# Preparation and edge pass of a four-layer graph network in one program, with five more slots for gathered rows

## The reference

```python
h = maximum(layernorm(x), 0)
msg_input = concatenate([h[src], h[dst], edge_attr], axis=-1)
m = relu(msg_input @ W1.T + b1) @ W2.T + b2
agg = segment_sum(m, dst)
y = h + relu(agg @ Wu.T + bu)
x = x + layernorm(y) * gamma + beta
```

## Time and profile before

| | us |
|---|---|
| median of 3 runs | 1938.01 (1937.61 to 1939.03) |
| the profiled execution, its span | 2170.3 |
| difference to the median | 232.3 |
| start of the gathers of PHL (POOL, L399) | 75.8 |
| end of VectorE's work in the preparation | 117.2 |
| first product of the edge pass (PE, L1309) | 128.5 |
| first and last gather of the edge pass (POOL, L989) | 130.6 and 1345.0 |

### The profile page before, as it was taken

One profiled execution on the slowest core, in us unless ns is written; L12 is line 12 of the kernel. 1 busy time (PEld: TensorE's weight loads), 2 busy tenths in 40 slices (PEclk: granted clock), 3 DMA queues, 4 the chain that ended last, 5 costly groups with the idle time before them and its releaser, 6 DMA issues. The chain is left out here.

```text
span 2170.3 us, 30067 instructions
## 1 busy us (share of the span) xinstructions
PE 1378.5 (64%) x9130; PEld 904.1 (42%) x9130; DVE 1129.6 (52%) x3500; ACT 812.2 (37%) x3272; POOL 841.7 (39%) x877
## 2 busy tenths in 40 slices
PE   3235444445445454545545445799899999899997
PEld 2123233333333333333333333356656666455444
DVE  7756666667667666666666666431442224311101
ACT  2235455555545555454545544111343432100000
POOL 5636666666666666666666665000000000000001
PEclk8566766666666666666665666899999999899999
DMA  6444434434443433434434443103100001871770
GB/s 198 143 96 116 115 113 116 122 115 121 121 116 112 122 120 114 118 113 122 119 112 117 120 119 103 30 12 139 34 29 1 10 7 39 305 266 65 264 293 29
DMA packets 200853, 245.67 MB, mean 113 GB/s; under 512 B 36794, under 2 KB 174053, under 8 KB 200674
## 3 DMA queue, kind: packets, MB, share of 16 engines
q1 hardware_dynamic: 142978, 137.56, 20.1%
q0 software_dynamic: 29472, 65.73, 11.7%
q10 hardware_dynamic: 28224, 40.15, 5.2%
HBM read 174.00 MB, written 55.93 MB: 106 GB/s over the span
## 5 line engine op out<-in xcount | busy, mean ns | idle before, releaser
L989 POOL DMA_INDIRECT arena<-dram_PHL,src_of x786 | 765.2, 974 | 472.1 <-remote 205.4
L1327 PE MATMUL psum<-arena 128*128 128x150 f16 x1568 | 238.9, 294 | 604.3 <-DVE aw_out L1034 330.4
L1327 PEld LDWEIGHTS psum<-arena 128*128 128x128 f16 x1568 | 153.4, 125 | 762.2 <-issue 380.6
L1228 ACT ACTIVATE arena<-psum 128x512 f16<-128x512 f32 x202 | 121.9, 603 | 429.3 <-remote 294.5
L1236 ACT ACTIVATE arena<-psum 128x150 fp8e4<-128x150 f32 (+1 forms) x588 | 173.6, 295 | 181.4 <-remote 93.8
L1241 ACT ACTIVATE arena<-psum,arena 128x150 f16<-128x150 f32 (+1 forms) x588 | 228.6, 389 | 1.6 <-remote 1.6
L1309 PE MATMUL psum<-arena 128*128 128x128 f16 x1612 | 182.2, 281 | 39.0 <-DMA arena<-dram_QHL 36.3
L1054 DVE SCALAR_TENSOR_TENSOR agg_all<-psum,agg_all 128x64 f32<-128x64 f32 x202 | 43.8, 217 | 283.4 <-remote 281.4
L1314 PE MATMUL psum<-arena 128*128 128x512 f16 x404 | 184.5, 552 | 3.6 <-issue 3.6
L1244 ACT ACTIVATE aw_out<-psum 128x150 f32<-128x150 f32 (+1 forms) x588 | 179.6, 305 | 0.0
L1043 DVE SCALAR_TENSOR_TENSOR arena<-psum,arena 128x512 f16<-128x512 f32 x202 | 137.9, 683 | 76.2 <-issue 41.3
(11 more groups left out here) (344 smaller groups left out, 2080.3 us busy)
## 6 DMA issues: line engine op xcount, KB each, us to landing
dram_aw<-aw_out ACTq DMA_DIRECT2D x196, 200.0 KB
arena<-dram_aw SPq DMA_DIRECT2D x6, 6400.0 KB
arena<-dram_aw SPq DMA_DIRECT2D x3, 4800.0 KB
arena<-in_ea_quads SPq DMA_DIRECT2D x51, 256.0 KB
arena<-dram_rel SPq DMA_DIRECT2D x51, 256.0 KB
arena<-arena SPq DMA_DIRECT2D x408, 32.0 KB
arena<-dram_PHL,src_of POOLq DMA_INDIRECT x806
arena<-dram_aw SPq DMA_DIRECT2D x2, 4000.0 KB
```

Of the source, the lines that this page charges most:

```text
L989: nc.gpsimd.indirect_dma_start(gathered_p[:, slot, k, :], None, d["PHL"], bass.IndirectOffsetOnAxis(ap=src_of[:, b:b + 1], axis=0)).then_i ...
L1327: done = nc.tensor.matmul(thirds[:, :, i * PKEY:(i + 1) * PKEY], hot_lo[:, u, p, :], hot_key[:, u, p], start=True, stop=True)
```

## The change

One block holds both parts: `prepare` returns five functions that `edge_pass` calls at the head of each engine's program, and the barriers between them are gone. The semaphores of the preparation live on. The preparation's buffers are laid out anew, in strips that the matrix of counts reaches only in later steps. Products and parts have three buffers, and `add_bias`, `copy_p` wait for the stores of group c - 3.

POOL's gathers have ten slots at the start: groups 0 to 4 and then 10, 11, ... use the five of before, groups 5 to 9 five more, once, over the memory of x after h0's stores have landed.

On VectorE `degrees` (in steps 0 to 5), `out_of_bands` (10, 11), `reach` (12, 13) and `badness` (14 to 21) are moved into the loop, each instruction waiting for the end of the one before (`linked`). The degrees are turned round by PE at step 5, stored and loaded back by SyncE at its step 4; folding is at step 8 in place of 2. `row_fields` works with one operation on `past` (f16) and one on the keys where there were two on the keys; `ea_low` comes earlier, `rel_of` is copied by ScalarE, and the squares of the weights come ahead of `ea_high`.

```diff
+AHEAD_P = 5
...
+    d["ahead_p"] = halves[:, H_FIRST:H_FIRST + AHEAD_P * slot].rearrange("p (a b f) -> p a b f", b=MB, f=2 * D)
...
+def slot_of(d, g):
+    if SLOTS_P <= g < SLOTS_P + AHEAD_P:
+        return d["ahead_p"][:, g - SLOTS_P]
+    return d["s_gathered_p"][:, g % SLOTS_P]
...
-        pq = sb("pq", [P, 2, GT, 2, D], F32)
-        hl = sb("pq_parts", [P, 2, GT, 2, 2, D], F16)
+    pq = sb("pq", [P, 3, GT, 2, D], F32)
+    hl = sb("pq_parts", [P, 3, GT, 2, 2, D], F16)
...
 # gpsimd, end of the preparation
-                for g in range(SLOTS_P):
-                    for k in range(blocks_of(g)):
-                        ...
-                pool.wait_ge(rows_in, 16 * PCOLS)
...
 # vector, row_fields
-                    step(nc.vector.tensor_scalar(rows[:, :, :, A_KEY], rows[:, :, :, A_KEY], base[:, 0:1], None,
-                                                 ALU.subtract))
-                    step(nc.vector.scalar_tensor_tensor(out=rows[:, :, :, A_KEY], in0=past[:, :, :], scalar=OUTSIDE,
-                                                        in1=rows[:, :, :, A_KEY], op0=ALU.mult, op1=ALU.add))
+            step(nc.vector.tensor_scalar(past, past, OUTSIDE, base[:, 0:1], ALU.mult, ALU.subtract))
+            dve.wait_ge(pair_rows, 16 * PCOLS)
+            step(nc.vector.tensor_tensor(rows[:, :, :, A_KEY], rows[:, :, :, A_KEY], past, ALU.add))
...
 # vector, end of the preparation's order
-                low_weights()
-                out_of_bands()
-                add_bias(6)
-                low_parts(6)
+        low_weights()
+        add_bias(6)
+        row_lengths()
+        low_parts(6)
...
+        row_fields()
+        ea_low(0)
+        for n, col in enumerate(range(1, PCOLS, 2)):
+            ...
+        ea_low(1)
...
-                degrees()
-                ea_low(0)
-                ea_low(1)
-                reach()
-                badness()
...
 # build
-        prepare(nc, new, d)
-        end_phase()
-        edge_pass(nc, new, d)
+        prepared = prepare(nc, new, d)
+        edge_pass(nc, new, d, prepared)
...
 # edge_pass
+        DEGREES, FOLD = 4, 8
...
 def gather(g):
-                    slot = g % NPG
-                    if g >= NPG:
-                        pool.wait_ge(pre, g - NPG + 1)
+                    if g == SLOTS_P:
+                        pool.wait_ge(d["h_stored"], 16 * G)
+                    if SLOTS_P + AHEAD_P <= g < 2 * SLOTS_P + AHEAD_P:
+                        pool.wait_ge(pre, g - SLOTS_P - AHEAD_P + 1)
+                    elif g >= 2 * SLOTS_P + AHEAD_P:
+                        pool.wait_ge(pre, g - SLOTS_P + 1)
...
-                for g in range(NPG, MG):
+                for g in range(MG):
                     gather(g)
...
 # sync, in the loop
+                    if s == DEGREES:
+                        store_degrees()
...
 # vector, in the loop, after low_parts(s), add(s - 1)
+                def left_over(s):
+                    if s == 0:
+                        weights_of_rows()
+                    if s == 1:
+                        count_of_first()
+                    if s == 2:
+                        weight_of_first()
+                    if s == 3:
+                        weights_of_both()
+                    if s == DEGREES:
+                        degrees_of_rows()
+                    if s == DEGREES + 1:
+                        degrees_out()
+                    if s in (10, 11):
+                        out_of_band(s - 10)
+                    if s == 12:
+                        most_of_weights()
+                    if s == 13:
+                        reach_of_weights()
+                    if s == 14:
+                        bad_order()
+                    if s in (15, 16):
+                        bad_weights(s - 15)
+                    if 17 <= s < 17 + PARTS_OF_ROW:
+                        sum_bad(s - 17)
+                    if s == 17 + PARTS_OF_ROW:
+                        sum_all_bad()
...
 # tensor, in the loop
+                    if s == DEGREES + 1:
+                        await_rows(s)
+                        turn_degrees()
-                    if s == 2:
+                    if s == FOLD:
                         await_rows(s)
                         fold_weights()
```

More of the change, by code:

```diff
@@ L145 @@
 SLOTS_P, BANDS_HELD = 5, 8
+AHEAD_P = 5
+ROW_T = NCOL // 2
+KEPT = 256
 def share_buffers(nc, d):
@@ new lines, in gathered_of, with strip @@
+def gathered_of(d, g):
+    if SLOTS_P <= g < SLOTS_P + AHEAD_P:
+        return d["gathered_ahead"][g - SLOTS_P], 16 * blocks_of(g)
+    before = [k for k in range(g % SLOTS_P, g + 1, SLOTS_P) if not SLOTS_P <= k < SLOTS_P + AHEAD_P]
+    return d["gathered"][g % SLOTS_P], 16 * sum(blocks_of(k) for k in before)
+def strip(d, row, rows, at, shape, dt):
+    size = 4 if dt in (F32, I32) else 2
+    flat = d["arena"][:, :, :].rearrange("p t n -> p (t n)")[0:shape[0], 0:NT * ROW_T]
+    if dt is not F16:
+        flat = flat.bitcast(dt)
+    view = flat.rearrange("p (t n) -> p t n", t=NT)[:, row:row + rows, at // size:at // size + math.prod(shape[1:])]
+    assert at % size == 0 and at + math.prod(shape[1:]) * size <= 2 * ROW_T
+    axes = [f"a{i}" for i in range(len(shape) - 1)]
+    sizes = {a: n for a, n in zip(axes[1:], shape[2:])}
+    return view.rearrange(f"p t ({' '.join(axes)}) -> p t {' '.join(axes)}", **sizes)
@@ L1162, in raise_flag, with linked @@
                     step(nc.vector.tensor_copy(d["flag"][:, :], row[:, 7:8]))
+                rows, past, w_slot, w_half, sums = d["rows"], d["past"], d["w_slot"], d["w_half"], d["sums"]
+                out_sum, norms, most, reach = d["out_sum"], d["norms"], d["most"], d["reach"]
+                per_dst, bad, bad_rows = d["per_dst"], d["bad"], d["bad_rows"]
+                left = [0]
+                def linked(ins):
+                    left[0] += 1
+                    ins.then_inc(left_step, 1)
+                    dve.wait_ge(left_step, left[0])
@@ new lines, in most_of_weights @@
+                def most_of_weights():
+                    dve.wait_ge(d["w_rooted"], 1)
+                    dve.wait_ge(d["w_in"], 64)
+                    b1 = d["b1_rows"]
+                    for a in range(3):
+                        nc.vector.reduce_max(most[:, a:a + 1], norms[:, a * D:(a + 1) * D], axis=AX.X)
+                    linked(nc.vector.scalar_tensor_tensor(out=norms[:, 3 * D:4 * D], in0=b1, scalar=-1.0, in1=b1,
+                                                          op0=ALU.mult, op1=ALU.max))
+                    linked(nc.vector.reduce_max(most[:, 3:4], norms[:, 3 * D:4 * D], axis=AX.X))
@@ L1311, in build @@
                                              stop=False)
[L1312 removed]
+                    pe.wait_ge(*gathered_of(d, g))
                     for part in range(2):
[L1314 removed]
+                        done = nc.tensor.matmul(out, ident_h[:, :], slot_of(d, g)[:, 0:n, part * D:(part + 1) * D],
                                                 start=False, stop=(part == 1))
```

1136 lines of the change are left out of this document (586 added, 550 removed).

## The result

The changed kernel takes 1907.91 us (median of 4 runs, 1906.35 to 1909.57); the kernel before, in the runs beside it, takes 1938.52 (4 runs, 1937.61 to 1941.23). The ratio is 0.984, 95% interval 0.9826 to 0.9854: 30.6 us faster, where 21.6 were forecast.

The account below looks back on a forecast made before the run. POOL's gather stream was taken to bound the edge pass. Idle stretch 17.8 plus earlier start 3.8, contention 0, gave 21.6 us off 1938.0: 1916 us; own range 1908 to 1923, 8 in 10 range 1903 to 1930.

Parts of the forecast that it names:

- The bound: Edge pass: POOL's gather stream sets the time, first gather at 75.8 us, 1.25 us for each of the rest.
- Rival A: Edge pass: the consumer (VectorE, PE, ScalarE) binds the timed runs too; 1898 to 1920 us; chance 0.12.
- The idle stretch: POOL's wait at the seam before the edge pass goes: 21.6 us against the profile, 17.8 against timed runs.
- The start: First gather of PHL: comes 3.8 us earlier, at 72, as group 6 is stored sooner; bounds 0 and 6.2.
- Slots and consumer: Seam: five more slots and first build at 85 to 90 leave no stall at group 15, 8 us in hand.
- B: Steps 5 to 22: linked moved work lengthens steps and the ring of slots bites; costs 12 us, 1928; chance 0.10.
- D: Steps with moved work: each pays 2.0 us more in lost turns; 25 to 29 us slower, 1965; chance 0.08.
- E: Seam: POOL sits waiting for h0's stores until the first builds, so the slots go unused; 1934; chance 0.06.
- the sign of a late consumer: Early edge pass: POOL waiting for PE near 130 us or at group 15 would show the forecast wrong.
- Length of the gathers: VectorE operations beside POOL's first gathers: stretching removed and added cancel, net 0, bounds -2.6 and +3.8 us.
- The page's rule: Two-port or two-SBUF-input VectorE operations and GpSimd operations exclude each other; in full, 3.8 us less gain, 1920.
- The tail: After the last gather: the time stays the same, 825 us.

Follow-up runs that it names:

- the pair of kernels with products and sums: Changed kernel plus 15 VectorE operations of 1.88 us, two-input products or one-input sums: 2158.25 and 2152.21 us, beside 2150.94 for the changed kernel on that chip.

## Why the prediction was right

- **The bound.** The gather stream sets the edge pass on a chip of the first kind: 80 gathers in each 100 us, 0.30 us between them. That was the claim and it holds. Its ground was half wrong. The stops without a named cause in the earlier trace rows belong to a kind of chip and not to the profiler. For the timed runs of that chip the conclusion was the same. Part of the support was luck: the 1933.7 of the prediction has 1.244 us for a gather, which are 1.265 on the first kind (16 us more over 786), and 825.3 us behind the last gather, which are 811.6 there (14 less), and the two errors mostly cancel. Rival A is out on the first kind, since in the loop of the changed kernel POOL's waits for PE are 1.8 us in all. On the other kind its condition holds (POOL waits for PE 87.6 us and stops for 175.4 by no named cause in the changed kernel), but not its price: the first build hardly moves (126.39 against 128.48 in the earlier trace rows), and the same change gives 0.3% and not 1.6%. In its sum the 39.7 us belong to a first build at 85; at 87 they are 37.7 (128.48 less 3.78 less 87), which moves A's range by 2 us and decides nothing.
- **The idle stretch.** Forecast 17.8 (21.6 less a stop of 3.8), measured 24.5. The step that failed is the stop: I took the edge pass to start as much earlier as VectorE ends earlier. VectorE did end sooner (113.2 against 117.2), but so did its degrees (105.3 against 109.3), and their stores now fell among POOL's last gathers. POOL's DRAIN held the barrier until 119.3, and the first load came at 120.9 where the earlier trace rows have 118.8. That term is 6.7 us short and is most of the miss of 9.0 (30.6 less 21.6).
- **The start.** Forecast 3.8, measured 1.9 (75.82 to 73.93). The parts of group 6 were made at 66.2, near the forecast, but their store was issued at 70.30: SyncE stood 3.82 us in issuing group 5's store, with a DMA share of 1.12 from 60 to 65 us, as in the earlier trace rows, and had four more stores to issue. The term was mis-sized by 1.9. Storing PHL first shows that 5.6 us lay there.
- **Slots and consumer.** The first build was forecast at 85 to 90 and came at 86.97. The build of step 5 came at 113.3 (119.5 forecast), that of step 11 at 141.4 (147), and POOL asked for group 15 at 154 (155) without waiting. The slow steps are there: PE's multiplication stood 4.88, 2.58 and 1.96 us for VectorE's `aw_out` at 101.04, 106.94 and 112.21. They had slack to spend, so rivals B and D did not come about. E is out too: the 21st gather, the first into the new slots, starts after 0.30 us. I gave the slots credit that they don't deserve: with the consumer that early, five do. On the second kind the sign of a late consumer did come, the wait at group 15, after stops that no rival named.
- **Length of the gathers.** Forecast 0 net (-2.6 to +3.8 of cost), measured a gain of 3.6. Above their usual 0.944 us the first 20 gathers held 8.2 us before and 3.5 after; the 54 after them 1.1 and 2.9, the rest 12.1 and 11.3. The moved operations of 1.88 us with two inputs stretch a gather each, as forecast, but the reductions, which are half of the work moved to steps 0 to 5, stretch none. `row_fields` got 1.6 of the 3.2 us: its operation on `past` takes 0.68 us (1.02 forecast), but its sum of two f16 inputs takes 3.82 us like the one before it, not 1.88. It hurt no gather, since it runs at 70.11, ahead of the stream.
- **The page's rule.** The Trainium skill's rule ("SBUF — State Buffer", on the shared port pair) is borne out in its mechanism by the row at 301.55 and the pair of kernels with products and sums. It limits the case of two inputs to a GpSimd operation that reads SBUF, which fits a gather (its places are in `src_of`, in SBUF). The charge of 3.8 us by it was not borne out, since the blocked issues that went away were more than those that came.
- **The tail** after the last gather: 811.6 and 811.0, unchanged as forecast.

Open: what stops the engines on the second kind of chip. A window of the loop there has 66 gathers in place of 80, with single operations as long as elsewhere (gathers 979 ns against 966) and a granted clock of 0.66 against 0.67:

```profile
500.00:600.00 100.00, 48.99 (x438) 36.15 (x435) 69.32 (x218) 52.44 (x239) 64.44 (x66) 0.66 0.43 120
```

No run here tells whether DMA, semaphores or the fetching of instructions is behind it. Also open is what storing PHL first gives where the stream is the bound; by the account above at most 5.6 us, to about 1902, which is an estimate.

## What to carry to other kernels

Find the one stream that has no gaps, and count a change by what it does to that stream: here the seam cost 24 us because POOL ran out of slots behind it, and either more slots or an earlier consumer closed the gap; both were not needed. Before costing a barrier, read each engine's own last instruction in front of it: this one was held by POOL's DRAIN, which small stores among its last gathers made 7 to 8 us longer, and not by the engine whose work ended last. Where a profile's span is far from the timed median, find out whether it is from another chip before explaining the difference away.

## What the runs showed of the hardware

- Two kinds of chips (or of sessions, see above), 1937 and 2157 us for the same program, and a change worth 1.6% on one and 0.3% on the other.
- An indirect DMA of 128 rows costs POOL 0.94 us and 0.30 to the next; if a VectorE operation with two SBUF inputs of 1.88 us runs, the issue ends 0.82 us after it. A reduction of 1.88 us has no such effect. A short operation with two SBUF inputs stretches less: beside one of 0.68 us (`ea_low`, 103.47 in the changed kernel) a gather takes 1.29 us and ends 0.81 us after it.
- A store can hold SyncE for 3.82 us in its issue while the DMA engines are full (share 1.12 from 60 to 65 us).
- POOL's DRAIN in front of a barrier ends 3.8 us after its last gather, and 10.6 to 11.7 us after it where four small stores are issued among the last gathers.
- Four stores of degrees issued from 105.4 to 108.4 in small pieces took 6.8 to 10.0 us to land, on DMA engines that moved only 27 GB/s at a share of 1.03 (window 108 to 114 above).
